# A state-space kernel on one core: GpSimd's product of C with an older state moves between the two halves of u times B

## The chip, the cores and the metric

The kernel runs on one core of one Trainium2 chip. The metric is device time in microseconds (us) of one execution. The engines are TensorE (PE; PEld is its weight load), VectorE (DVE), ScalarE (ACT), GpSimd (POOL) and SyncE (SP), whose queue issues the DMAs.

## The reference, cut to what matters

A layer norm of x (8 x 1024 tokens of 512) feeds a feed-forward part with fp4 rounding, which runs first and isn't touched, and a selective state-space (Mamba) part, which is the subject here. Its core is

```python
def step(h, inp):
    xt, dtt, Bt, Ct = inp
    dA = jnp.exp(dtt[:, :, None] * A[None])
    h = h * dA + (dtt * xt)[:, :, None] * Bt[:, None, :]
    y = jnp.einsum('bds,bs->bd', h, Ct)
    return (h, y)
```

with 1024 channels d, 16 states s and 1024 steps per sequence. Around it are an input projection, a convolution over 4 taps, a SiLU gate with z and an output projection; x and the feed-forward result are added.

## The kernel before

The state-space part is `phase_b`. Tokens are cut into 16 **chunks** of 512; two chunks make one sequence, so the first of a pair starts from state 0 (`hs<-decay,v` in the rows) and the second from a kept state (`hs<-decay,carry,v`). The two chunks of one pass of a hardware loop are called even and odd here. Chunks 0, 1, 14 and 15 are written out; 2 to 13 are six passes of the loop on every engine.

A chunk is 32 **slots** k = 0 to 31: 2 groups of 512 channels times 16 states. A slot is 4 **steps** n = 4k + j, one for each block of 128 channels. What each engine does, in an order fixed in the program:

- **GpSimd**, slot k (`drive`, L1184 to L1195): `v[k % 2]` = u times B, in two instructions of two blocks each (L1193), called the low half (j = 0, 1) and the high half (j = 2, 3) here. The low half waits for the row of B (`b_rep`, three buffers) and for scans 0 and 1 of slot k - 2, the high half for scans 2 and 3 of that slot. Then `weigh` (L1197 to L1205): `hw` = state of slot k - 2 times C for the last 128 tokens of the chunk (L1203), for 28 of the 32 slots (`WEIGHED`: not for 5, 9, 27 and 29). Last, in 10 of the slots, the steps of `POOL_AT`: in slots 3 and 4 `y2` (L1218, `sz<-acc,sz`) of the chunk before, in slots 7, 11, 29 and 31 `sp` (L1222) and `du` (L1228), in 22 and 23 `y2` of this chunk.
- **ScalarE**, step n: `decay` = exp(A dt) into one of three PSUM buffers (L1392), and between these the copies and functions of `ACT_AT`, among them the copy of `yt` (L1324) at step 13.
- **VectorE**, step n: the scan over 512 tokens (L1434), then for n - 5 the sum `acc` += turned state times C (L1448), where the state isn't weighed by GpSimd. The scan of step 4k waits until state buffer k % 3 is free: its old state must be turned by TensorE and multiplied by GpSimd (`weighed`). The old state is that of slot k - 3, but **at the head of a chunk that of slot 30 (for k = 0) and 31 (for k = 1)** of the chunk before, only two slots back. GpSimd multiplies these two in its slots 0 and 1.
- **TensorE**, step n: it turns state n - 4 (`ht`, L1579), then adds up a product of C (`yw`, L1589) of slot (n - 9)/4, then does its share of the projections by a list (`MM`). At step 10 comes `yt(1, 0)` (L1557), which needs `y2` of GpSimd's slot 3.
- **SyncE**: slot k issues the steps of `SP_AT`, then the row of C for slot k (L1089), then the row of B for slot k + 2 (L1083), which waits for both halves of v of the slot that used its buffer last. Slot 31 first issues `x_z` (L1118, 1 MB), which waits for TensorE, and then the B row of the next chunk's slot 1.

Of the kernel before, what the change touches and what calls it, by code (L numbers as in the profile page):

```python
# [821 lines left out]
def phase_b(nc, ctx, xn_d, xnt, res, ssm_d, tap_d, xc_d, halo_d, ident, out, W_in, conv_w, conv_b, W_x, A_log, D_param, dt_bias, W_out):  # L822
# [18 lines left out]
    NC, KH, CL = xnt.shape[0], xnt.shape[2], xnt.shape[3]  # L841
    DI, NS = A_log.shape
    D = W_out.shape[1]
    ND, GD, NT, KC = DI // P, 4, CL // P, conv_w.shape[2]
# [132 lines left out]
    def sums(c, k, t):  # L977

        return c.at(ADDS, max(i for (a, b), i in add_no.items() if b == t and a <= k) + 1)
# [18 lines left out]
    def whose(c, what, g=None):  # L998

        if what == "tr":  # L1000
            return c.plus(2)
        if what == "tr_late":
            return c.plus(1)
        if what in ("ip", "cv", "ssm", "ct", "silu_xc"):
            return c.plus(1)
        if what in ("abs", "exp", "ln", "relu", "sp", "du", "xd"):
            return c if g == 1 else c.plus(1)
        if what in ("wo", "yt", "y2", "silu_z", "add", "load", "store"):
            return c.plus(-1) if g == 1 else c
        return c  # L1010

    def is_first(o):

        return isinstance(o.q, int) and o.c == 0

    def wait(eng, sem_, value):

        if not isinstance(value, int) or value > 0:
            eng.wait_ge(sem_, value)  # L1019

    def over_chunks(eng, part, first=-1):

        for r in range(first, 2):
            part(Chunk(0, r))
        with eng.Fori(1, NC // 2 - 1) as q:
            part(Chunk(q, 0))
            part(Chunk(q, 1))
        for r in (0, 1, 2):
            part(Chunk(NC // 2 - 1, r))
# [151 lines left out]
    @block.gpsimd  # L1181
    def _(pool):

        def drive(c, k):  # L1184

            g = k // NS
            for j in range(0, GD, 2):
                if j == 0:
                    wait(pool, b_loaded[k % 3], c.at(16 * len(range(k % 3, SLOTS, 3)), 16 * (k // 3) + 16))
                if k % NS == 0:  # L1190
                    wait(pool, u_ready, c.at(8, 4 * g + j + 2))
                wait(pool, scanned, c.at(128, 4 * (k - 2) + j + 2))
                nc.gpsimd.tensor_tensor(v[k % 2][:, j:j + 2, :], u[g][:, j:j + 2, :],  # L1193
                                        b_rep[k % 3][:, :].unsqueeze(1).broadcast_to([P, 2, CL]),
                                        ALU.mult).then_inc(v_ready, 2)  # L1195

        def weigh(c, k):  # L1197

            w = weigh_no[k]
            wait(pool, c_loaded[w % 4], c.at(4 * NW, 16 * (w // 4) + 16))  # L1200
            wait(pool, w_turned, c.at(NW, w - 1))
            wait(pool, scanned, c.at(128, 4 * k + 4))
            nc.gpsimd.tensor_tensor(hw[w % 2][:, :, :], h[k % 3][:, :, LT * P:],  # L1203
                                    c_rep[w % 4][:, :].unsqueeze(1).broadcast_to([P, GD, P]),
                                    ALU.mult).then_inc(weighed, 1)  # L1205

        def extra(c, what, g, half):
            o = whose(c, what, g)
            if not o.exists(NC) or (what in ("sp", "du") and g == 0 and is_first(o)):
                return  # L1210
            j = 2 * half
            two = slice(j, j + 2)
            if what == "y2":
                wait(pool, z_ready, o.at(4, 2 * g + half + 1))
                wait(pool, summed, sums(o, NS * g + NS - 1, j + 1))
                if half == LT // 2:
                    wait(pool, yw_added, o.at(2, g + 1))
                nc.gpsimd.tensor_tensor(sz[:, two, :], acc[g][:, two, :], sz[:, two, :], ALU.mult).then_inc(y2_ready, 2)  # L1218
            elif what == "sp":
                wait(pool, sp_ops, o.at(16, 8 * g + 7 + half))  # L1220
                wait(pool, relu_set, o.at(8, 4 * g + j + 2))
                nc.gpsimd.tensor_tensor(dt[g][:, two, :], dt[g][:, two, :], u[g][:, two, :], ALU.add).then_inc(dt_ready, 2)  # L1222
            else:
                wait(pool, xc_ready, o.at(ND, GD * g + j + 2))
                if is_first(o):
                    pool.wait_ge(xc0_loaded[2], 16)
                wait(pool, dt_ready, o.at(8, 4 * g + j + 2))
                nc.gpsimd.tensor_tensor(u[g][:, two, :], dt[g][:, two, :], xc[:, GD * g + j:GD * g + j + 2, :],  # L1228
                                        ALU.mult).then_inc(u_ready, 2)

        def part(c):
            for k in range(SLOTS):
                if c.exists(NC):
                    drive(c, k)
                done, m = (c, k - 2) if k >= 2 else (c.plus(-1), k + SLOTS - 2)
                if done.exists(NC) and m in weigh_no:
                    weigh(done, m)
                for what in POOL_AT.get(k, ()):
                    extra(c, *what)

        over_chunks(pool, part)

    @block.scalar
# [410 lines left out]
```

## Time and profile before

| what | value |
|---|---|
| median of 3 runs | 5356.45 us (5354.84 to 5357.74) |
| the profiled execution | 5352.76 us, its span 5351.0 us |
| PE busy | 4918.7 us, 92% |
| DVE busy | 4686.7 us, 88% |
| POOL busy | 3950.9 us, 74% |
| ACT busy | 2777.2 us, 52% |

The feed-forward part takes the first 1750 us or so; there GpSimd is busy little. In the state-space part behind it, VectorE and GpSimd are each busy over 95% of the time. Rows of a timeline give the start in us from the span's start, the length in us, engine, line, operation, what it writes from what it reads, and in brackets the engine's idle time before it with what ended it. "x2" is two instructions in one row.

### The profile page before, as it was taken

The numbers are of one execution on the slowest core, as the hardware profiler recorded it, in microseconds if no ns is written. First come the engines' busy times: TensorE is split into PE (matmuls) and PEld (weight loads), VectorE is DVE, ScalarE is ACT, GpSimd is POOL, SyncE is SP. The second block draws the span as 40 slices with busy tenths as digits, with TensorE's granted clock in tenths as the row PEclk, the third lists the DMA queues.
The fourth block names the chain that finished last, engine by engine and source line by source line (L and its number), as shares of the span: only waits on it lengthen the run. The fifth ranks groups of instructions, "written<-read, shape, count | busy, mean of one in ns | idle before, by whom it ended". The sixth has DMA issues, their size and how long they took to land.

```text
span 5351.0 us, 80535 instructions
## 1 busy us (share of the span) xinstructions
PE 4918.7 (92%) x22532; PEld 3287.7 (61%) x22532; DVE 4686.7 (88%) x5835; ACT 2777.2 (52%) x4594; POOL 3950.9 (74%) x2047
## 2 busy tenths in 40 slices
PE   5899999999999799899999999989999999999967
PEld 2688888888888455555555555555555555555544
DVE  9676766767676699999999999999999999999997
ACT  3111111111111576777677677777667776767754
POOL 5233333333332599999999999999999999999996
PEclk9999999999999899999999999999999999999979
DMA  4111111111110423323233333333333333323222
GB/s 117 48 44 41 45 39 45 41 43 43 39 47 32 128 88 111 102 92 108 87 122 101 91 104 110 98 102 94 115 95 99 107 92 111 110 81 114 80 91 66
DMA packets 286369, 444.72 MB, mean 83 GB/s; under 512 B 39521, under 2 KB 100961, under 8 KB 281746
## 3 DMA queue, kind: packets, MB, share of 16 engines
q1 hardware_dynamic: 285970, 440.23, 26.2%
q8 instruction: 150, 2.46, 0.2%
q14 instruction: 249, 2.04, 0.1%
HBM read 350.94 MB, written 89.17 MB: 82 GB/s over the span
## 4 chain that ended last, share of the span: by engine, by line
DVE 18%; PE 17%; issue 14%; ACT 8%; POOL 7%; DVEq 1%; DMA 1%; SPq 0%; POOLq 0%; ACTq 0%
DVE hs L1434 11%; DVE acc L1448 6%; POOL v L1193 5%; PE mm L1567 4%; PE ht L1579 4%; ACT decay L1392 3%; PE mm L1508 3%; PE mm L1499 3%; PE mm L1516 2%; POOL hw L1203 1%; PE yw L1589 1%; PE mm L1551 1%; DVEq L1019 1%; DMA b_rep<-ssm_d 1%; ACT L1279 1%
## 5 line engine op out<-in xcount | busy, mean ns | idle before, releaser
L1193 POOL TENSOR_TENSOR v<-u,b_rep 128x1024 f32<-128x1024 f32 x1024 | 2401.2, 2365 | 150.2 <-DVE hs L1434 68.1
L1392 ACT ACTIVATE decay<-dt,a_neg 128x512 f32<-128x512 f32 x2048 | 1389.7, 688 | 657.0 <-DVE hs L1434 644.7
L1579 PEld LDWEIGHTS ht<-ident,hs 128*128 128x128 f32 x6400 | 784.8, 144 | 1013.9 <-issue 662.6
L1434 DVE TENSOR_TENSOR_SCAN hs<-decay,carry,v 128x512 f32<-128x512 f32 x1024 | 1285.2, 1273 | 34.9 <-POOL hw L1203 19.5
L1434 DVE TENSOR_TENSOR_SCAN hs<-decay,v 128x512 f32<-128x512 f32 x1024 | 1230.6, 1221 | 49.2 <-ACT decay L1392 38.3
L1448 DVE SCALAR_TENSOR_TENSOR acc<-ht,c_now,acc 128x512 f32<-128x512 f32 x1600 | 1173.3, 733 | 17.4 <-PE ht L1579 16.5
L1579 PE MATMUL ht<-ident,hs 128*128 128x128 f32 x6400 | 1005.0, 281 | 179.3 <-DVE hs L1434 83.6
L683 ACT ACTIVATE sg<-gate 128x512 f32<-128x512 f32 (+1 forms) x192 | 108.1, 563 | 1339.9 <-PE up L723 1339.9
L1203 POOL TENSOR_TENSOR hw<-hs,c_rep 128x512 f32<-128x512 f32 x448 | 572.1, 1277 | 10.4 <-DVE hs L1434 10.4
L1567 PE MATMUL mm<-w_out,yt 128*128 128x512 f32 x1024 | 513.0, 605 | 8.7 <-ACT xb L1264 5.2
L1516 PE MATMUL mm<-w_in,x_z 128*128 128x512 f32 x1024 | 508.6, 601 | 6.7 <-ACT acc L1318 6.7
L1499 PE MATMUL mm<-x_in,w_in 128*128 128x512 f32 x960 | 484.2, 613 | 3.1 <-ACT x_in L1286 2.7
L1508 PE MATMUL mm<-xb,tap_diag 128*128 128x512 f32 x960 | 467.0, 596 | 6.1 <-ACT rtb L1314 6.1
L106 POOL TENSOR_TENSOR h<-h,h_small 128x1408 f32<-128x1408 f32 x64 | 166.2, 2597 | 413.8 <-DVE h_small L100 413.8
L151 POOL TENSOR_TENSOR h<-h,h_small 128x1408 f32<-128x1408 f32 x64 | 166.4, 2600 | 335.3 <-DVE h L145 335.3
L1589 PE MATMUL yw<-ident,hw 128*128 128x128 f32 x1792 | 283.5, 283 | 57.6 <-DVE acc L1456 46.6
L721 PE MATMUL gate<-gu,xqt 128*128 128x512 f32 (+1 forms) x768 | 301.4, 392 | 5.8 <-DVE xqt L619 5.8
L628 DVE TENSOR_TENSOR rt<-down,rt 128x512 f32<-128x512 f32 x64 | 44.3, 692 | 297.8 <-PE down L723 297.8
L722 PE MATMUL gate<-gu,xqt 128*128 128x512 f32 (+1 forms) x768 | 289.9, 378 | 0.0
L723 PE MATMUL gate<-gu,xqt 128*128 128x512 f32 (+1 forms) x768 | 289.5, 377 | 0.0
L721 PE MATMUL up<-gu,xqt 128*128 128x512 f32 (+1 forms) x768 | 288.7, 376 | 0.0
L723 PE MATMUL up<-gu,xqt 128*128 128x512 f32 (+1 forms) x768 | 288.7, 376 | 0.0
(157 smaller groups left out, 7971.0 us busy)
## 6 DMA issues: line engine op xcount, KB each, us to landing
b_rep<-ssm_d SPq DMA_DIRECT2D x512, 256.0 KB, 3.5
w_out<-in_L_attn_W_out SPq DMA_DIRECT2D x32, 1024.0 KB, 7.8
rtb<-res_d SPq DMA_DIRECT2D x128, 256.0 KB, 4.1
tap_diag<-tap_d SPq DMA_DIRECT2D x120, 256.0 KB, 3.5
c_rep<-ssm_d SPq DMA_DIRECT2D x448, 64.0 KB, 3.4
xt<-in_L_attn_x SPq DMA_DIRECT2D x64, 256.0 KB, 2.7
xn_d<-xn SPq DMA_DIRECT2D x64, 256.0 KB, 2.0
rt<-in_L_attn_x SPq DMA_DIRECT2D x64, 256.0 KB, 2.6
```

The source lines that it names most:

```text
L721: nc.tensor.matmul(out, left_hi, right_hi, start=(k == 0), stop=False)
L723: last = nc.tensor.matmul(out, left_lo, right_hi, start=False, stop=(k == len(pairs) - 1))
L1193: nc.gpsimd.tensor_tensor(v[k % 2][:, j:j + 2, :], u[g][:, j:j + 2, :], b_rep[k % 3][:, :].unsqueeze(1).broadcast_to([P, 2, CL]), ALU.mult ...
L1203: nc.gpsimd.tensor_tensor(hw[w % 2][:, :, :], h[k % 3][:, :, LT * P:], c_rep[w % 4][:, :].unsqueeze(1).broadcast_to([P, GD, P]), ALU.mult) ...
L1392: nc.scalar.activation(decay[n % 3][:, :], dt[g][:, j, :], ACT.Exp, scale=a_neg[:, GD * g + j, s:s + 1]).then_inc(decay_ready, 1)
L1434: nc.vector.tensor_tensor_scan(h[k % 3][:, j, :], decay[n % 3][:, :], v[k % 2][:, j, :], carry[:, s, GD * g + j:GD * g + j + 1] if c.secon ...
L1448: nc.vector.scalar_tensor_tensor(out=acc[g][:, t, :], in0=ht[add_no[k, t] % 2][:, :, :].rearrange("p j d -> p (j d)"), scalar=c_now[c.r % ...
L1499: made, done = nc.tensor.matmul(bank[:, :], w_in[:, k, i * P:(i + 1) * P], x_in[:, k, :], start=first, stop=last), ip_done
L1508: made, done = nc.tensor.matmul(bank[:, skip:], tap_diag[i % 2][:, tap, :], xb[i % 2][:, tap + skip:tap + CL], start=first, stop=last), cv ...
L1516: made, done = nc.tensor.matmul(bank[:, :], x_z[:, k, t * P:(t + 1) * P], w_in[:, k, DI + g * GW:DI + (g + 1) * GW], start=first, stop=las ...
L1567: made, done = nc.tensor.matmul(bank[:, :], left, right, start=first, stop=last), wo_done
L1579: last = nc.tensor.transpose(ht[add_no[k, t] % 2][:, j, :], h[k % 3][:, j, t * P:(t + 1) * P], ident[:, :])
```

## The change

GpSimd's slot was low half, high half, product with C. It becomes low half, product with C, high half. Nothing is added or left out, and the waits of each instruction are the same as before.

```diff
-        def drive(c, k):
+        def drive(c, k, halves=(0, 1)):
             g = k // NS
-            for j in range(0, GD, 2):
+            for j in (2 * half for half in halves):
...
                 if c.exists(NC):
-                    drive(c, k)
+                    drive(c, k, (0,))
                 done, m = (c, k - 2) if k >= 2 else (c.plus(-1), k + SLOTS - 2)
                 if done.exists(NC) and m in weigh_no:
                     weigh(done, m)
+                if c.exists(NC):
+                    drive(c, k, (1,))
                 for what in POOL_AT.get(k, ()):
                     extra(c, *what)
```

## Rows read from the trace of the kernel before

**Rows 1.** Busy time in a stretch, with instruction counts, clock and DMA.

```profile
core 0: us, PE busy (x) PEld busy (x) DVE busy (x) ACT busy (x) POOL busy (x), PEclk, DMA share, GB/s
3100.00:3700.00 600.00, 553.80 (x2496) 324.77 (x2495) 584.20 (x631) 425.63 (x700) 578.72 (x286) 0.99 0.33 104
```

**Rows 2.** Waits, 1900 to 5100 us: total us, times, longest us.

```profile
DVE hs L1434 <- ACT decay L1392: 38.9, 35, 3.3
DVE hs L1434 <- POOL hw L1203: 22.7, 14, 2.7
DVE acc L1448 <- PE ht L1579: 8.9, 24, 1.2
DVE hs L1434 <- PE ht L1579: 8.9, 6, 2.0
SPq L1118 <- PE mm L1516: 152.2, 15, 11.3
```

**Rows 3.** GpSimd's instructions by line: busy us, mean ns, idle before.

```profile
L1193 POOL TENSOR_TENSOR v<-u,b_rep 128x1024 f32<-128x1024 f32 x1024 | 2401.2, 2365 | 150.2 <-DVE hs L1434 68.1 <-DVE u L1420 34.1 <-DMA b_rep<-ssm_d 29.1
L1203 POOL TENSOR_TENSOR hw<-hs,c_rep 128x512 f32<-128x512 f32 x448 | 572.1, 1277 | 10.4 <-DVE hs L1434 10.4
```

**Rows 4.** Timeline of GpSimd, slots 0, 1 and 3 of chunk 7.

```profile
3332.19 4.68 POOL L1193 TENSOR_TENSOR v<-u,b_rep 128x1024 f32<-128x1024 f32 x2
3336.82 1.27 POOL L1203 TENSOR_TENSOR hw<-hs,c_rep 128x512 f32<-128x512 f32 x1
3340.35 4.70 POOL L1193 TENSOR_TENSOR v<-u,b_rep 128x1024 f32<-128x1024 f32 x2 [2.26 <-DMA b_rep<-ssm_d]
3345.01 1.26 POOL L1203 TENSOR_TENSOR hw<-hs,c_rep 128x512 f32<-128x512 f32 x1
...
3357.95 2.37 POOL L1218 TENSOR_TENSOR sz<-acc,sz 128x1024 f32<-128x1024 f32 x1
```

**Rows 5.** Timeline of VectorE, same stretch: head of chunk 7, then step 13.

```profile
3335.57 0.74 DVE L1448 SCALAR_TENSOR_TENSOR acc<-ht,c_now,acc 128x512 f32<-128x512 f32 x1
3338.37 2.46 DVE L1434 TENSOR_TENSOR_SCAN hs<-decay,carry,v 128x512 f32<-128x512 f32 x2 [2.06 <-POOL hw L1203]
...
3346.55 2.46 DVE L1434 TENSOR_TENSOR_SCAN hs<-decay,carry,v 128x512 f32<-128x512 f32 x2 [1.41 <-POOL hw L1203]
...
3363.28 0.75 DVE L1448 SCALAR_TENSOR_TENSOR acc<-ht,c_now,acc 128x512 f32<-128x512 f32 x1 [0.32 <-PE ht L1579]
```

**Rows 6.** Timeline of TensorE, same stretch: steps 10 to 12.

```profile
3360.46 0.63 PE L1557 MATMUL mm<-ident,sz 128*128 128x128 f32 x4 [1.53 <-POOL sz L1218]
3360.92 1.88 PE L1499 MATMUL mm<-x_in,w_in 128*128 128x512 f32 x4
3362.64 0.60 PE L1579 MATMUL ht<-ident,hs 128*128 128x128 f32 x4
```

**Rows 7.** Timeline of SyncE's queue at the same chunk boundary.

```profile
3332.59 0.33 SPq L1118 DMA_DIRECT2D x_z<-xnt_d  x1
3333.10 0.33 SPq L1089 DMA_DIRECT2D c_rep<-ssm_d  x1
3333.75 0.33 SPq L1083 DMA_DIRECT2D b_rep<-ssm_d  x1
```

**Rows 8.** Timeline at chunk 15: VectorE at steps 0 and 14, ScalarE at step 13.

```profile
5099.75 2.46 DVE L1434 TENSOR_TENSOR_SCAN hs<-decay,carry,v 128x512 f32<-128x512 f32 x2 [2.05 <-PE ht L1579]
...
5121.79 0.60 ACT L1324 ACTIVATE yt<-mm 128x512 f32<-128x512 f32 x1 [2.32 <-PE mm L1557]
...
5124.63 1.28 DVE L1434 TENSOR_TENSOR_SCAN hs<-decay,carry,v 128x512 f32<-128x512 f32 x1 [0.40 <-ACT decay L1392]
```

**Rows 9.** Timeline of VectorE, head of chunk 8, where the loop jumps back.

```profile
3558.55 0.73 DVE L1448 SCALAR_TENSOR_TENSOR acc<-ht,c_now,acc 128x512 f32<-128x512 f32 x1
3562.34 2.34 DVE L1434 TENSOR_TENSOR_SCAN hs<-decay,v 128x512 f32<-128x512 f32 x2 [3.06 <-ACT decay L1392]
```

**Rows 10.** Timeline of GpSimd, TensorE and VectorE in slot 12 of chunk 8.

```profile
3643.77 1.27 POOL L1203 TENSOR_TENSOR hw<-hs,c_rep 128x512 f32<-128x512 f32 x1
3645.00 4.67 POOL L1193 TENSOR_TENSOR v<-u,b_rep 128x1024 f32<-128x1024 f32 x2
3645.10 0.66 PE L1589 MATMUL yw<-ident,hw 128*128 128x128 f32 x4 [0.28 <-POOL hw L1203]
...
3645.61 1.21 DVE L1434 TENSOR_TENSOR_SCAN hs<-decay,v 128x512 f32<-128x512 f32 x1
...
3651.74 0.75 DVE L1448 SCALAR_TENSOR_TENSOR acc<-ht,c_now,acc 128x512 f32<-128x512 f32 x1 [0.26 <-PE ht L1579]
...
3655.63 0.75 DVE L1448 SCALAR_TENSOR_TENSOR acc<-ht,c_now,acc 128x512 f32<-128x512 f32 x1 [0.24 <-PE ht L1579]
```

## The prediction

> **What bounds the kernel now.** I read the busy time by stretch first, to see which engines have no room in the state-space part; then the list of waits there, to see what the fullest engine waits for; then timelines around those waits, to see what comes next if one goes. In a stretch of 600 us VectorE is busy for 584.2 and GpSimd for 578.7 [rows 1]. VectorE sets the pace: whatever removes its 2.6% of idle time, and that alone, shortens the kernel. Of the idle time in 1900 to 5100 us, 22.7 us in 14 waits are put down to GpSimd's product `hw`, 38.9 to ScalarE's decay and 8.9 twice to TensorE's turned states [rows 2]. The scan waits put down to `ht`, 8.9 us, are the same thing under another name: in chunk 15 the scan of step 0 waits 2.05 us [rows 8], and it stands at the place where the wait for `hw` stands in chunk 7. So some 31.6 us lie behind the product of C. All of it is at the head of a chunk.
>
> **The waits at the head.** In chunk 7 VectorE's last sum begins at 3335.57 and takes 0.74, so it is free at 3336.31. GpSimd's slot 0 begins at 3332.19: two halves, then the product of slot 30, from 3336.82 to 3338.09. Scan 0 starts at 3338.37, after 2.06 us idle [rows 4, 5]. The semaphore takes 3338.37 - 3338.09 = 0.28. Scan 4 waits 1.41 us in the same way for the product of slot 31, which ends at 3346.27 [rows 4, 5].
>
> **What the change moves.** Two starts of GpSimd's instructions, 3332.19 and 3336.82, are 4.63 us apart, so a half costs 2.32; the product costs 1.23 by the starts 3643.77 and 3645.00 [rows 4, 10]. Its mean span is 1.28 [rows 3]. The slot's sum is the same, so GpSimd's slots begin when they began. Within a slot `hw` is ready 2.32 us earlier and the high half of v 1.23 us later.
>
> A sentence on the choice between 1.23 and 1.28: the Trainium skill, page "Perfetto Trace Analysis", section "GPSIMD Instruction", says that a GpSimd span isn't to be trusted and that starts should be compared. The trace agrees so far as the starts give the smaller number; with 1.28 in place of 1.23 the spare time below would be 0.05 us less, and the sum the same.
>
> **First part, the heads, and why I cost the gain at nothing.** New order in chunk 7: low half 3332.19 to 3334.5, product of slot 30 to 3335.8, plus 0.28 is 3336.0, before VectorE is free at 3336.31. So scan 0 gains 2.1 us. GpSimd's slot 1 can't start before 3340.35, since it waits 2.26 us for its row of B [rows 4]; its product now ends at 3340.35 + 2.32 + 1.27 = 3343.9. VectorE gets scan 4 at 3344.2, 2.3 us earlier than 3346.55, still after a wait of about 1.3. If nothing else held it, every such head would give 2.3 us.
>
> What is late next: `y2` in GpSimd's slot 3. It stands behind the whole of slots 1 to 3, so it runs from 3357.95 to 3360.32 as before. TensorE has been idle 1.53 us for it when it starts `yt(1, 0)` at 3360.46; then come four projection matmuls, and the turned state of slot 2 is finished at 3362.64 + 0.60 = 3363.24. VectorE's sum of step 13 starts at 3363.28, after an idle time of 0.32 us that ends with it [rows 4 to 6]. That chain is bound to the row of B in slot 1, and it holds VectorE already now. With VectorE 2.3 us ahead it waits 0.32 + 2.3 = 2.6 us there and goes on at 3363.28 as before. The gain of each head is handed back 13 steps later: 0. The same small wait stands at step 13 in chunks 1, 2, 3, 5, 7, 9, 13 and 14, from 0.26 to 1.2 us (they are most of the 8.9 us and hold the longest of the 24 waits of sums [rows 2]); in chunk 11 the turned state comes just in time.
>
> Chunk 15 has no such wait for the turned state, but a second tail of the same chain: ScalarE waits 2.32 us for `yt` of TensorE, then does its step 13, and scan 14 waits 0.40 us for its decay [rows 8]. So it is 0 there too.
>
> Where the loop jumps back (heads of chunks 4, 6, 8, 10 and 12), VectorE is idle for 3.06 us [rows 9] and the product isn't what ends it; moving the product brings 0.
>
> **Second part, slot 12 of the even chunks.** TensorE's `yw` waits 0.28 us for `hw` of slot 10 at 3645.10 (the product ended at 3645.04). VectorE's sums of steps 53 and 55 then wait 0.26 and 0.24 us for turned states [rows 10]. With `hw` 2.32 us earlier TensorE doesn't wait and is 0.3 to 0.45 us ahead, so the first of the two goes, and the second perhaps. The pair stands in chunks 2, 4, 8, 10 and 12, among the same 24 waits [rows 2]. Bounds: from 0 (another chain ends at the same time) to 0.50 a chunk. I take 0.3, nearer to the first wait's 0.26: 5 x 0.3 = 1.5 us gained.
>
> **Third part, the later high half.** It delays two users. The scans: the tightest place is slot 12 of an even chunk. Its high half ends with the pair, when `hw` starts: 3643.77 + 0.04 = 3643.81. Scan 50 starts at 3645.61 [rows 10]. 1.80 us are spare, of which 1.23 are used and 0.57 are left: cost 0. It can't bring a gain, since nothing here becomes ready sooner.
>
> The other user is SyncE, whose load of a row of B waits for the high half; behind it in the same queue are the row of C, the tap loads, residual rows, `x_z` and `w_out`. The row that GpSimd waits for at the head of each chunk is issued at 3333.75, right behind the 1 MB of `x_z` at 3332.59 [rows 7], and `x_z` has waited for TensorE for 152.2 us in 15 times, 10 us each [rows 2]. So 1.23 us later in the queue ahead of it is covered by those 10 us: cost 0. If that cover were gone it would cost 1.23 a chunk.
>
> **Sum.** 5352.76 (profiled execution, 1.8 over its span) - 0 - 1.5 + 0 = 5351.3. The median of the runs is 3.7 us above the profiled execution; I take the 1.5 off the median: 5356.45 - 1.5 = 5355.0.
>
> **The rivals.**
>
> *The heads' gain is kept (faster).* Ten heads (chunks 1, 2, 3, 5, 7, 9, 11, 13, 14 and 15) give up to 2.32 each, of the 31.6 us or so that are waited: 23 us, 5356.45 - 23 - 1.5 = 5332. For it: the waits for `hw` are the largest that the change touches, and they do go. Against it: `y2` and its 1.53 us of TensorE idle, and the 0.32 us at step 13, which show that the chain through GpSimd's slots 1 to 3 is late already. It would need that chain to begin earlier, that is, the row of B to land earlier. A part of it, if the row lands some 0.5 us earlier because `w_out` is issued later behind it: 10 x 0.5 = 5 us, 5350.
>
> *The rows of B come later (slower).* SyncE gets past its loads 1.23 us later in each slot. If this reaches the load for slot 1, GpSimd's slot 1, `y2`, the turned state and step 13 all shift by 1.23: 15 heads x 1.23 = 18.5 us, 5356.45 + 18.5 = 5375. It decides from the point where SyncE reaches `x_z` less than 1.23 us before TensorE is done; the row says 10 us.
>
> *The high half comes too late for scans 2 and 3 (slower).* It needs GpSimd's slots to be 0.57 us behind by slot 12. Slots 1 to 12 run back to back, so 0.05 us more in each slot would do it. At 0.1 a slot it would cost 0.6 us in each of 7 even chunks, 4 us: 5359. Against it: each slot has the same three kinds of hand-over between instructions as before (half to half, half to product, product to half), only in another order.
>
> **How the numbers follow.** Nothing much changes (5350 to 5360): 0.80. Heads' gain kept, wholly or by more than 11 us: 0.10; in a small part: 0.03. Rows of B late: 0.04. High half late: 0.03. A measurement of this kernel can tell about 0.2%, 10.7 us, from no change. Faster by more than that 0.10; slower by more 0.04, to which I add 0.02 for a high half later than worked out; within it 0.84. The range takes in the likeliest case with its bounds (0 to 2.5 us gained), 3 to 5 us of scatter, since the three runs lie 2.9 us apart, the small part of the first rival and the third: 5345 to 5362. The wholly kept gain and the late rows of B, 0.14 together, lie outside.
>
> **What would show it.** VectorE's waits put down to `hw` fall from 22.7 to below 10 us, and those of its sums for turned states grow from 8.9 to 25 or more, at step 13. In chunk 7, scan 0 follows the last sum without a gap, and scans from step 14 on stand as before relative to the end of `y2`. TensorE's wait for `y2` in that head grows from 1.53 to about 3.8 us. The two waits in slot 12 of chunk 8 shrink. GpSimd's wait for the row of B stays near 2.3. I am wrong if sums at step 13 don't wait longer (then the heads' gain is real), or if scans 2 of some slot wait for `v`.

## The result, and the profile after

The changed kernel is slower by a little. Its median is 5365.62 us (5361.79 to 5371.34, 22 runs) against 5356.29 us (5354.04 to 5357.80, 22 runs) for the kernel before: 9.3 us more, a ratio of 1.0018 with a 95% interval of 1.0011 to 1.0024. The slowdown is real, since the interval leaves out 1, and it lies just within the 0.2% that the prediction called no change. The predicted time of 5355.0 and its range of 5345 to 5362 miss it. The profiled execution took 5365.12 us, its span 5363.3 us, 12.3 us more than the span before.

Lines of the kernel after stand two further down, except GpSimd's: scans are L1436, sums L1450, turned states L1581, `yt` L1559.

First the busy time in the same stretch as [rows 1]. Both full engines lose about a microsecond in 600, and TensorE's granted clock falls from 0.99 to 0.98.

```profile
core 0: us, PE busy (x) PEld busy (x) DVE busy (x) ACT busy (x) POOL busy (x), PEclk, DMA share, GB/s
3100.00:3700.00 600.00, 553.19 (x2491) 325.18 (x2490) 583.03 (x629) 425.37 (x699) 577.88 (x285) 0.98 0.32 103
```

Then the waits of 1900 to 5100 us, as in [rows 2] (total us, times, longest us).

```profile
DVE acc L1450 <- PE ht L1581: 42.7, 11, 5.7
DVE hs L1436 <- ACT decay L1394: 39.6, 38, 3.2
PE mm L1559 <- POOL sz L1218: 38.9, 14, 4.1
DVE hs L1436 <- POOL hw L1203: 7.9, 9, 1.4
DVE hs L1436 <- PE ht L1581: 3.0, 2, 1.5
SPq L1118 <- PE mm L1518: 123.7, 14, 10.0
```

VectorE's scans waited 22.7 us for `hw` and 8.9 us for `ht` [rows 2]; now they wait 7.9 and 3.0. Of the 8.9, 5.9 us stood at heads and are the same event under another name; 3.0 us stand at step 88 of chunks 0 and 14, in both kernels. Its sums waited 8.9 us for turned states in 24 times; now they wait 42.7 us in only 11. The waits moved, as forecast, and grew on the way: 28.6 us for the product and 8.9 us for turned states became 7.9 us and 42.7 us. TensorE's wait for `y2` in the same stretch, 38.9 us, was this before:

```profile
PE mm L1557 <- POOL sz L1218: 18.7, 14, 2.0
```

Timeline of VectorE after, chunk 7, which answers to [rows 5]: the chunk's head and step 13. The head lies 5.1 us later in this execution than before, so only differences count.

```profile
3340.68 0.74 DVE L1450 SCALAR_TENSOR_TENSOR acc<-ht,c_now,acc 128x512 f32<-128x512 f32 x1
3341.32 2.46 DVE L1436 TENSOR_TENSOR_SCAN hs<-decay,carry,v 128x512 f32<-128x512 f32 x2
...
3349.34 2.46 DVE L1436 TENSOR_TENSOR_SCAN hs<-decay,carry,v 128x512 f32<-128x512 f32 x2 [1.25 <-POOL hw L1203]
...
3369.97 0.75 DVE L1450 SCALAR_TENSOR_TENSOR acc<-ht,c_now,acc 128x512 f32<-128x512 f32 x1 [4.22 <-PE ht L1581]
```

Timeline of GpSimd after, same head, which answers to [rows 4].

```profile
3345.47 2.37 POOL L1193 TENSOR_TENSOR v<-u,b_rep 128x1024 f32<-128x1024 f32 x1 [2.27 <-DMA b_rep<-ssm_d]
3347.80 1.26 POOL L1203 TENSOR_TENSOR hw<-hs,c_rep 128x512 f32<-128x512 f32 x1
...
3363.07 2.33 POOL L1218 TENSOR_TENSOR sz<-acc,sz 128x1024 f32<-128x1024 f32 x1
```

Timeline of TensorE after, same head, which answers to [rows 6].

```profile
3365.54 1.08 PE L1559 MATMUL mm<-ident,sz 128*128 128x128 f32 x4 [3.82 <-POOL sz L1218]
3366.42 3.08 PE L1501 MATMUL mm<-x_in,w_in 128*128 128x512 f32 x4
3369.33 0.60 PE L1581 MATMUL ht<-ident,hs 128*128 128x128 f32 x4
```

Read in this order they tell the whole case. Scan 0 follows the last sum with no gap (2.06 us before), scan 4 waits 1.25 us (1.41 before). GpSimd's slot 1 waits for its row of B as before, 2.27 us, and `y2` begins 3363.07 - 3345.47 = 17.60 us behind it, where [rows 4] give 3357.95 - 3340.35 = 17.60. So the chain that the prediction named begins no later and runs no slower up to `y2`. Behind `y2` it is slower. From the start of `yt(1, 0)` to the start of the turned state it is 3369.33 - 3365.54 = 3.79 us, where it was 3362.64 - 3360.46 = 2.18 [rows 6]. The same four instructions of `yt` take 1.08 us in place of 0.63 and the four of the projection 3.08 in place of 1.88.

The reason stands in the clock. First the kernel before, while TensorE waits for `y2` and right behind it:

```profile
3358.90:3360.40 1.50, 0.03 (x1) 0.00 (x0) 1.50 (x2) 1.50 (x3) 1.50 (x2) 1.00 0.76 210
3360.40:3362.60 2.20, 2.14 (x8) 1.21 (x9) 2.20 (x3) 1.42 (x3) 2.20 (x2) 1.00 0.05 18
```

and the kernel after, the same two stretches (the column behind POOL is the granted clock):

```profile
3361.50:3365.50 4.00, 0.22 (x3) 0.00 (x0) 4.00 (x5) 1.69 (x3) 4.00 (x3) 0.99 0.15 47
3365.50:3369.30 3.80, 3.76 (x8) 2.06 (x9) 0.25 (x1) 2.58 (x4) 3.80 (x3) 0.56 0.25 91
```

After an idle time of 1.5 us the matmuls ran at 1.00, which is 2.4 GHz; after 3.8 us they ran at 0.56, which is 1.2 GHz for nearly all of the stretch. VectorE was busy for 0.25 us of it: the slow matmuls lie on the path.

The ten heads where the product held VectorE, read from the two traces. "Waits" is the sum of VectorE's idle times ahead of scan 0, scan 4 and the sum of step 13 (in chunk 15 ahead of scan 14 too); "idle" is TensorE's idle time ahead of `yt(1, 0)`; "clock" is the granted clock in the 3.5 us behind it.

| chunk | waits before | after | idle before | after | clock before | after |
|---|---|---|---|---|---|---|
| 1 | 3.24 | 5.52 | 1.66 | 3.96 | 1.00 | 0.64 |
| 2 | 4.09 | 6.49 | 1.82 | 4.05 | 1.00 | 0.50 |
| 3 | 3.59 | 5.41 | 1.48 | 3.83 | 1.00 | 0.64 |
| 5 | 3.81 | 5.47 | 1.54 | 3.83 | 1.00 | 0.57 |
| 7 | 3.79 | 5.47 | 1.53 | 3.82 | 1.00 | 0.53 |
| 9 | 3.65 | 6.65 | 1.55 | 3.85 | 1.00 | 0.50 |
| 11 | 2.83 | 4.55 | 1.18 | 3.38 | 1.00 | 0.57 |
| 13 | 3.40 | 4.73 | 1.52 | 3.58 | 1.00 | 0.51 |
| 14 | 4.13 | 6.06 | 2.02 | 3.97 | 1.00 | 0.50 |
| 15 | 2.47 | 2.57 | 0.96 | 3.24 | 0.50 | 0.50 |
| sum | 35.0 | 52.9 | | | | |

The heads cost 17.9 us more in this execution and the span grew by 12.3. Two things went the other way. In slot 12 of the even chunks, of the two waits [rows 10] the first is gone and the second is 0.10 us, 5 x 0.40 = 2.0 us. And the first scan of the state-space part starts at 1790.8 us in place of 1792.1, 1.3 us earlier, ahead of all that the change touches. Some 2 us remain spread over the kernel, the size by which runs of one kernel differ. The heads of the even chunks 4 to 12, where the loop jumps back, didn't change: TensorE idles there 0.6 to 1.2 us ahead of `yt`, the clock behind it stays at 1.00, and VectorE still waits some 3 us for its first decay.

### The profile page after: what moved, and what is told of

The parts are those of the page before. It is cut to its first block, busy times and chain, and to the rows that moved or that the text cites. A ratio compares the mean times of both kernels' runs of the same rounds, so it can differ in the third digit from the quotient of the medians.

```text
span 5363.3 us, 80211 instructions
## 1 busy us (share of the span) xinstructions
PE 4922.6 (92%) x22532; PEld 3294.3 (61%) x22532; DVE 4683.5 (87%) x5835; ACT 2776.7 (52%) x4594; POOL 3952.4 (74%) x2047
## 4 chain that ended last, share of the span: by engine, by line
DVE 20%; PE 18%; issue 13%; ACT 8%; POOL 4%; DMA 1%; DVEq 1%; SPq 0%; ACTq 0%; POOLq 0%
DVE hs L1436 13%; DVE acc L1450 7%; PE ht L1581 4%; PE mm L1569 4%; PE mm L1501 3%; ACT decay L1394 3%; PE mm L1510 3%; POOL v L1193 2%; PE mm L1518 1%; DMA b_rep<-ssm_d 1%; PE yw L1591 1%; PE mm L1553 1%; DVEq L1019 1%; POOL hw L1203 1%; ACT L1281 1%
## 5 line engine op out<-in xcount | busy, mean ns | idle before, releaser
L1581 PEld LDWEIGHTS ht<-ident,hs 128*128 128x128 f32 x6400 | 787.7, 144 | 1012.4 <-issue 675.3
L1436 DVE TENSOR_TENSOR_SCAN hs<-decay,carry,v 128x512 f32<-128x512 f32 x1024 | 1285.1, 1273 | 19.1 <-ACT decay L1394 12.3
L1436 DVE TENSOR_TENSOR_SCAN hs<-decay,v 128x512 f32<-128x512 f32 x1024 | 1226.4, 1215 | 45.0 <-ACT decay L1394 38.8
L1450 DVE SCALAR_TENSOR_TENSOR acc<-ht,c_now,acc 128x512 f32<-128x512 f32 x1600 | 1168.2, 730 | 54.0 <-PE ht L1581 52.9
L1581 PE MATMUL ht<-ident,hs 128*128 128x128 f32 x6400 | 1004.6, 281 | 178.2 <-DVE hs L1436 82.6
```

The lines of the kernel that those rows point to most:

```text
L1436: nc.vector.tensor_tensor_scan(h[k % 3][:, j, :], decay[n % 3][:, :], v[k % 2][:, j, :], carry[:, s, GD * g + j:GD * g + j + 1] if c.secon ...
L1450: nc.vector.scalar_tensor_tensor(out=acc[g][:, t, :], in0=ht[add_no[k, t] % 2][:, :, :].rearrange("p j d -> p (j d)"), scalar=c_now[c.r % ...
L1581: last = nc.tensor.transpose(ht[add_no[k, t] % 2][:, j, :], h[k % 3][:, j, t * P:(t + 1) * P], ident[:, :])
```

## The experiments

**The theories.** *The clock theory*: the gain of the heads is handed back through `y2`, as predicted, and on top TensorE, which now idles 3.8 us for `y2`, does `yt` and the projection at half the clock, which costs 1.6 us and more in each of nine heads. *The first rival*: the chain of GpSimd itself is later, through rows of B or hand-overs. The trace speaks against it (17.60 in both). *The second rival*: the loss comes from the later high halves all over the chunk. In the expectations "theory" is the clock theory unless the words beside it name another. The kernel before ran beside each group of kernels with medians from 5355.74 to 5355.76 us; ratios are against it.

### Which slots carry the loss

**e2_heads_only**: the new order only in slots 0 and 1, which do the products of slots 30 and 31.

```diff
+                split = k < 2
                 if c.exists(NC):
-                    drive(c, k, (0,))
+                    drive(c, k, (0,) if split else (0, 1))
...
-                if c.exists(NC):
+                if split and c.exists(NC):
                     drive(c, k, (1,))
```

> The new order in slots 0 and 1 alone, the old order in all others. Nothing is left out. Theory (clock, at the heads): all of the loss is made there, and the gain of slot 12 is missing: 5365.6 + 2 = 5367 to 5369 us, sums at step 13 wait 4.2 us as in the changed kernel. Rival (the later high half or the later loads of rows cost in the other 30 slots): 5356 us or a little less.

Measured: 5368.37 us (5366.68 to 5372.62), ratio 1.0025 (1.0016 to 1.0035), as expected. The whole loss is there with two slots of 32 changed.

**e3_all_but_heads**: the same edit with `split = k >= 2`, the new order in the other 30 slots.

> The old order in slots 0 and 1, the new one in the other 30. Nothing is left out. Theory (clock, at the heads): no loss, and slot 12 of the even chunks gives 0.3 to 0.5 us in five chunks: 5354 us (5353 to 5355.5), TensorE waits for y2 as before (1.5 us in chunk 7). Rival (the other slots make the loss): 5362 us or more.

Measured: 5356.07 us (5353.05 to 5359.35), ratio 0.9999 (0.9990 to 1.0008). No loss is there; the small gain that was expected, 5353 to 5355.5, isn't seen either. The waits of the two kernels stand apart as they should. First e2_heads_only:

```profile
DVE acc L1451 <- PE ht L1582: 45.4, 18, 5.8
PE mm L1560 <- POOL sz L1218: 39.2, 14, 4.1
```

then e3_all_but_heads:

```profile
DVE hs L1437 <- POOL hw L1203: 23.7, 14, 3.4
PE mm L1560 <- POOL sz L1218: 19.5, 14, 2.0
DVE acc L1451 <- PE ht L1582: 8.7, 16, 1.2
```

The second is the kernel before in all three rows ([rows 2] have 22.7 and 8.9, and TensorE's wait was 18.7). So the later high halves of 30 slots cost nothing, and the second rival falls. VectorE has no wait left in slot 12 of chunk 8 in e3_all_but_heads, but the 1.5 us that this should bring can't be told from the scatter of runs.

### Is it the clock?

If the clock is the cause, TensorE at work while it waits should take the loss away, even if the work is useless. It costs nothing as long as it ends before `y2` does.

**e1_fill6**: six matmuls into the bank that `yt(1, 0)` is about to overwrite, in every head, ahead of the wait for `y2`.

```diff
             bank, first, last = mm[n % 2], unit == 0, unit == UNITS[what] - 1
+            if what == "yt" and args == (1, 0):
+                for i in range(6):
+                    nc.tensor.matmul(bank[:, :], ident[:, :], w_in[:, i % KH, 0:512], start=True, stop=True)
```

> The changed kernel, and TensorE does six extra matmuls (identity times a 128x512 piece of w_in, into the PSUM bank that yt(1, 0) writes right after) before it waits for y2 at step 10. Nothing is left out. Theory (clock): the changed kernel loses its time because TensorE's wait for y2 grows from 1.53 to 3.82 us and the granted clock behind it is 0.56 in place of 1.00, which makes the yt and projection matmuls of that head about 1.6 us longer. With six matmuls (2.6 us) in the wait the clock stays at 1.00 there, the sum of step 13 waits 2.6 us and not 4.2, and nine to ten heads give back 1.6 us each: 5365.6 - 15 = 5351 us. Rival (the chain through GpSimd is itself later, by its order or by the DMA of the row of B): the clock of TensorE doesn't matter, 5365 us.

Measured: 5386.69 us (5383.26 to 5387.78), ratio 1.0056 (1.0043 to 1.0070). A miss, and the timeline of TensorE in chunk 7 tells why:

```profile
3370.50 5.32 PE L1497 MATMUL mm<-w_in,ident 128*128 128x512 f32 x12
3375.65 0.60 PE L1562 MATMUL mm<-ident,sz 128*128 128x128 f32 x4
```

Each of these 32-bit matmuls stands as two instructions in the trace (x12 for six), so they take 5.32 us and not half of it. They fill the wait and run past it, in the heads of even chunks too, where only 0.6 to 1.2 us were free: at step 13 of chunks 4, 6, 8, 10 and 12 VectorE now waits 4.0 us each, 20 us, where it waited 0.3 at most. That is most of the 21 us by which this kernel is slower than the changed one. The clock behind the fill did stay at 1.00. The time says nothing on the theory, so the size was changed.

**e5_fill3_odd**: three matmuls, and only in odd chunks (`and c.second` added to the condition, `range(3)`).

> As e1, but three extra matmuls (e1's trace: twelve instructions in 5.32 us for six, so 2.7 us for three) and only at the heads of odd chunks, where the changed kernel's TensorE waits 3.2 to 3.9 us for y2. Nothing is left out. Theory (clock): TensorE is idle about 1.2 us in place of 3.8, its clock stays at 1.00, the sum of step 13 waits 2.6 us and not 4.2 or more; seven heads give back 1.6 us, chunks 2 and 14 are left as they are: 5365.6 - 11.5 = 5354 us (5352 to 5357). Rival (the chain itself is later in the changed kernel): 5365 us.

Measured: 5359.82 us (5357.03 to 5362.60), ratio 1.0008 (0.9999 to 1.0017). Windows of chunk 7, the wait with the fill and the stretch behind it:

```profile
3360.80:3364.60 3.80, 2.75 (x8) 0.97 (x6) 3.80 (x5) 1.65 (x3) 3.80 (x2) 1.00 0.13 41
3364.70:3367.20 2.50, 2.49 (x11) 1.48 (x12) 0.30 (x1) 1.73 (x3) 2.50 (x2) 1.00 0.41 147
```

and rows of TensorE and, last, VectorE at step 13:

```profile
3364.71 0.66 PE L1562 MATMUL mm<-ident,sz 128*128 128x128 f32 x4 [1.16 <-POOL sz L1218]
3365.21 1.88 PE L1504 MATMUL mm<-x_in,w_in 128*128 128x512 f32 x4
...
3367.56 0.75 DVE L1450 SCALAR_TENSOR_TENSOR acc<-ht,c_now,acc 128x512 f32<-128x512 f32 x1 [2.56 <-PE ht L1584]
```

The projection takes 1.88 us again. VectorE's wait at step 13 is 2.56 us, where the prediction had said 2.6 and the changed kernel has 4.22. It is 2.56 to 2.58 in all six odd chunks from 3 to 13. The heads of chunks 2 and 14, which were not, still wait 4.71 and 5.96 us at a clock of 0.55 and 0.50. In chunk 15 the fill changes little: its waits sum to 2.32 us in place of 2.57.

The time is a miss all the same: 5352 to 5357 was expected, and 5.8 us came back in place of 11.5. The heads aren't where it is missing. Their waits sum to 41.4 us by the trace, in place of 52.9, so they give back the 11.5. Two other places took some of it in this execution. Chunk 0, which has no fill, is 3.0 us longer than in the changed kernel's profile (e3_all_but_heads and e7_b_first show the same 3 us there, so it hangs on no fill; its cause is open). And in chunks 5, 7, 11 and 13 VectorE waits 0.4 to 0.7 us for a turned state at step 75; the kernel before has such waits in chunks 9, 11 and 13.

**e9_fill3_sel**: the three matmuls in the odd chunks up to 13 and in 14, and not in 15.

```diff
+            filled = (c.c in (1, 13, 14)) if isinstance(c.q, int) else c.second
+            if what == "yt" and args == (1, 0) and filled:
```

> As e5, but the three extra matmuls stand at the heads of the odd chunks 1 to 13 and of chunk 14, and not at the head of chunk 15. Nothing is left out. e5 came out at 5359.8, above what I expected; its trace puts the rest at the heads without cover (sum of step 13 waits 4.71 us in chunk 2 and 5.96 in chunk 14) and at chunk 15, where the matmuls came on top. Theory (the clock is all of the loss): chunk 14 gives back 1.7 to 2.6 us and chunk 15 about 2.5, chunk 2 stays: 5359.8 - 4.5 = 5355.3 us, no difference from the kernel before. Rival (a part of the loss has another cause, spread over the heads): 5359 us or more.

Measured: 5357.86 us (5351.70 to 5359.99), ratio 1.0002 (0.9993 to 1.0011). Its slowest run is below the fastest of the changed kernel, 5361.79. Twenty-four useless matmuls, three in each of eight heads, take the loss away as far as runs can tell. That is the direct evidence for the clock: nothing else was changed, the clock behind `yt` is 1.00 in all eight heads, and the wait at step 13 is 2.1 to 2.9 us in the seven odd ones, where 2.6 was forecast. It is also what the prediction's sum describes: all of the heads' gain handed back and nothing more. The time lies between the 5355.3 of the theory and the 5359 of its rival, so a part of up to 2 us with another cause isn't excluded. The head of chunk 2, which has no fill, accounts for 1.3 us of it: its waits sum to 5.3 us in place of 4.1 before. Between e5_fill3_odd and e9_fill3_sel the runs show no difference that can be told.

### Shortening TensorE's wait for y2

The theory says that the gain of the heads is real but is stopped at `y2`. Then `y2` earlier should set it free, and in the kernel before, where VectorE is held by the product first, it should bring little.

**e4_y2_slot2** moves the first `y2` from GpSimd's slot 3 to its slot 2 in the changed kernel, and **e6_y2_slot2_old** does so in the kernel before.

```diff
-    POOL_AT = {3: [("y2", 1, 0)], 4: [("y2", 1, 1)], 7: [("sp", 1, 0), ("du", 1, 0)],
+    POOL_AT = {2: [("y2", 1, 0)], 4: [("y2", 1, 1)], 7: [("sp", 1, 0), ("du", 1, 0)],
```

> The changed kernel, and the first y2 of the chunk before stands in GpSimd's slot 2 in place of 3, so 5.9 us earlier. Nothing is left out. Theory (the chain row of B, GpSimd's slots 1 to 3, y2, TensorE, step 13 hands the heads' gain back): TensorE doesn't wait for y2, its clock doesn't fall, the 2.3 us of ten heads are kept and the waits of 0.3 to 1.2 us at step 13 go too: 5356.3 - 23 - 3 - 1.5 = 5329 us (5325 to 5336). Rival (something else ends at the same time as y2, ScalarE's decay of step 14 or the scans' v, now 2.3 us later in slot 3): 5350 us or more.

> The kernel before, and the first y2 of the chunk before stands in slot 2 in place of 3, as in e4, without the changed order. Nothing is left out. Theory: the waits for the products of slots 30 and 31 (2.1 and 1.4 us in chunk 7) stay, since nothing there moves; only the waits at step 13 go, 0.26 to 1.2 us in eight heads, 3.9 us in all: 5355.8 - 4 = 5352 us. So e4's 26 us need both. Rival (e4's gain is that of y2 alone): 5330 us.

Measured: e4_y2_slot2 5329.65 us (5327.82 to 5331.43), ratio 0.9952 (0.9939 to 0.9966), and e6_y2_slot2_old 5351.56 us (5349.73 to 5355.70), ratio 0.9993 (0.9984 to 1.0002). Both times are as expected, though the 4 us of the second can't be told from no change. Waits of e4_y2_slot2, 1900 to 5100 us:

```profile
DVE hs L1436 <- POOL hw L1203: 9.2, 9, 1.3
DVE hs L1436 <- POOL v L1193: 7.3, 17, 0.7
DVE acc L1450 <- PE ht L1581: 0.7, 1, 0.7
```

and of e6_y2_slot2_old:

```profile
DVE hs L1434 <- POOL hw L1203: 23.8, 14, 3.2
DVE acc L1448 <- PE ht L1579: 8.4, 19, 1.2
```

In the new order the waits of VectorE's sums for turned states fall from 42.7 to 0.7 us. A new small one comes, 7.3 us for `v`. None of its 17 waits is near `y2`: they stand in slots 5, 8 and 12, and 13 of them are at a scan 2, which reads the high half. VectorE keeps its 2.3 us now, and it catches up with GpSimd. That fits the later high half beginning to count, whose cost was rightly put at 0 while the gain was handed back; no run here has the early `y2` without the later high halves and without the early row, so it isn't shown. In e8_y2_slot2_b_first below, where GpSimd is earlier too, no wait for `v` is left. In the old order the waits for `hw` stay at 23.8. There the waits at step 13 go wholly, as expected, but those of steps 53 to 55 and 75 to 77 grow, so that the sum is 8.4 us where it was 8.9.

### Taking away the wait for the row of B

**e7_b_first**: SyncE issues slot 31's row of C and the row of B for the next slot 1 ahead of `x_z`, which waits 10 us for TensorE, instead of behind it. So the chain itself begins earlier.

```diff
-             31: [("row", 3), ("x_z",)]}
+             31: [("row", 3)]}
...
                     load_b(c.plus(1), k + 2 - SLOTS)
+                if k == SLOTS - 1:
+                    move(c, "x_z")
```

> The changed kernel, and SyncE issues the rows of slot 31's C and of the next chunk's slot 1 of B before the 1 MB of x_z, not behind it. Nothing is left out. Theory (the chain begins with the landing of the row of B): GpSimd doesn't wait 2.3 us in slot 1, so slots 1 to 3 and y2 are 2.3 us earlier, TensorE waits 1.5 us for y2 and keeps its clock; the odd heads and those of 2 and 14 keep their gain: 5355.8 - 10 x 2.3 = 5333 us, and up to 1 us a head less for the wait for the product of slot 31: 5325 to 5335. Rival (the wait for the row of B isn't the start of the chain, another wait takes its place): 5350 us or more.

Measured: 5331.90 us (5326.50 to 5333.68), ratio 0.9952 (0.9938 to 0.9965), a time as expected. Its waits:

```profile
DVE acc L1452 <- PE ht L1583: 14.4, 16, 2.7
POOL v L1195 <- DMA b_rep<-ssm_d: 10.8, 14, 1.5
DVE hs L1438 <- POOL hw L1205: 0.4, 1, 0.4
```

GpSimd waits 10.8 us for rows of B where it waited 29.1 [rows 3]. With it goes scan 4's wait for `hw`, since that product stands in slot 1 behind the low half that the row had held up. The mechanism is only in part as expected. TensorE idles 2.3 us for `y2` in most odd chunks, where 1.5 were expected, and it doesn't keep its clock everywhere: VectorE waits 1.06 us at step 13 of chunks 3, 5 and 7, but 2.45 and 2.70 us in chunks 9 and 11. More on these two below.

**e10_b_first_old**: the same edit in the kernel before.

> The kernel before, and the rows of slot 31's C and of the next slot 1's B before x_z, as in e7, without the changed order. Nothing is left out. Theory: scan 0 still waits 2 to 2.7 us for the product of slot 30; the wait of scan 4, 0.3 to 1.4 us, falls to 0.5 or less; y2 is 2.3 us earlier, so step 13 doesn't hold VectorE: about 1 us for each of ten heads, 5355.7 - 10 = 5346 us (5342 to 5349), 14 us slower than e7. Rival (the row of B makes all of e7's gain, the order none): 5332 us.

Measured: 5338.37 us (5334.04 to 5340.97), ratio 0.9964 (0.9952 to 0.9976). A miss by 8 us: the earlier row is worth 17 us without the new order, not 10. By the trace two waits go, and they sum to 15 us, while scan 0's waits grow by 1 us in all. The rest of the 17 isn't accounted for. Scan 4's wait is gone in every head: 10.5 us in nine heads, of which chunks 2 and 14 alone had 2.73 and 1.74. And the row of B set the time of `y2` in this order as well, so the waits at step 13 went with it, 4.4 us; of the sums' waits of 8.9 us in all, 2.8 are left.

### Both, and the order's worth beside them

**e8_y2_slot2_b_first** has both edits on the changed kernel, **e11_y2_slot2_b_first_old** both on the kernel before, **e12_heads_y2_b** is the first with the new order only in slots 0 and 1.

> e4 and e7 together: the changed kernel, y2 in slot 2, the row of B before x_z. Nothing is left out. Theory: what e4 left at the odd heads is the wait of scan 4 for the product of slot 31, 0.8 to 1.6 us; with the row of B landed it falls to the 0.5 us of ScalarE's decay of step 5: 5329.7 - 8 x 0.7 = 5324 us. Rival (the row of B doesn't matter once y2 is early): 5330 us.

> e8 with the old order of GpSimd's slot: y2 in slot 2 and the row of B before x_z on the kernel before. Nothing is left out. Theory: the order alone makes the difference to e8, 2 to 2.3 us at each of ten heads: 5321.8 + 20 to 23 = 5343 us (5340 to 5346). Rival (the order is worth nothing once the chain is out of the way): 5322 to 5325 us.

> e8 with the new order in slots 0 and 1 alone, the old one in the other 30. Nothing is left out. It asks what the order is worth away from the heads. Theory (slot 12 of five even chunks gives 0.3 us each, the second part of the prediction): 5321.8 + 1.5 = 5323.3 us. Rival 1 (nothing): 5321.8. Rival 2 (the later high halves in e8 cost something by now): 5319 or less.

Measured: e8_y2_slot2_b_first 5321.83 us (5320.31 to 5322.88), ratio 0.9935 (0.9921 to 0.9948), 2 us better than expected. e11_y2_slot2_b_first_old 5338.97 us (5334.23 to 5340.48), ratio 0.9967 (0.9954 to 0.9979), a miss: 5340 to 5346 was expected. e12_heads_y2_b 5323.62 us (5321.88 to 5324.76), ratio 0.9939 (0.9926 to 0.9953), as expected. Waits of e8_y2_slot2_b_first, 1900 to 5090 us:

```profile
DVE acc L1452 <- PE ht L1583: 4.6, 10, 0.7
DVE hs L1438 <- POOL hw L1205: 1.0, 2, 0.5
```

and of e11_y2_slot2_b_first_old:

```profile
DVE hs L1436 <- POOL hw L1205: 14.2, 6, 2.7
DVE hs L1436 <- PE ht L1581: 7.5, 5, 2.0
DVE acc L1450 <- PE ht L1581: 3.1, 7, 0.7
```

With `y2` and the row out of the way the products still hold VectorE at the heads of the old order. Of the 7.5 us, 3.0 stand at step 88 of chunks 0 and 14 as in the kernel before; 4.5 and the 14.2 are at heads, 18.7 us. The new order leaves 1.0 us of them (its waits for `ht`, 4.2 us, are all at step 88). That is 17.7 us by the trace and 17.1 by the runs. The expectation had taken 20 to 23, 2 to 2.3 us a head; scan 0 waits that long in seven heads but only 0.8 to 1.7 us in chunks 1, 2 and 14. e8_y2_slot2_b_first is the best version, 34 us below the kernel before. The 1.8 us between it and e12_heads_y2_b fit the 1.5 us of slot 12, but they are no more than runs of one kernel differ by.

Medians in us, all eight together:

| | as it was | `y2` in slot 2 | row of B first | both |
|---|---|---|---|---|
| old order | 5356.29 | 5351.56 | 5338.37 | 5338.97 |
| new order | 5365.62 | 5329.65 | 5331.90 | 5321.83 |
| new minus old | +9.3 | -21.9 | -6.5 | -17.1 |

The same edit costs 9 us or brings 22, by what is late behind it. In the column where `y2` alone is earlier it brings 21.9 us, where the rival "the heads' gain is kept" has 23 and 1.5 for slot 12. That rival had priced the gain nearly rightly, and the waits for `v` may be what is missing. What it lacked was its condition, a `y2` that isn't late.

## Why the prediction was wrong, point by point

**What bounds the kernel, and the waits at the head: right.** VectorE's waits for the product are the ones that the change touches, and all are at heads. e2_heads_only and e3_all_but_heads show it from both sides. The working had two readings wrong, neither of which enters the sum: the waits for the product are 28.6 us and not 31.6, since 3.0 of the scans' waits for `ht` stand at step 88; and the waits at step 13 are 4.3 us of the 8.9, not most of them, the rest being 2.8 in slot 12, 1.7 at step 75 and 0.2 at step 13 of chunk 12.

**What the change moves: right.** `hw` is ready 2.3 us earlier in its slot: it starts 3347.80 - 3345.47 = 2.33 us behind the low half, where it was 4.66 [rows 4]. Scan 0's wait went wholly in chunk 7, and no head keeps more than 0.5 us of it. Scan 4 waits 1.25, where the working had 1.3.

**What is late next: right in place, wrong in size.** The chain over the row of B, slots 1 to 3, `y2`, `yt(1, 0)` and the turned state of step 13 takes the gain. TensorE's wait for `y2` grew from 1.53 to 3.82 us, where 3.8 was forecast. The step that failed is the sentence "With VectorE 2.3 us ahead it waits 0.32 + 2.3 = 2.6 us there and goes on at 3363.28 as before" and the 0 made of it. It took the time from `yt` to the turned state as a constant of 2.2 us, which it is only at the clock that TensorE had in [rows 6]. The idle time of 3.8 us was forecast, but not what TensorE does right behind it. It ran at half the clock, and the wait was 4.22 us: 0.32 + 2.3 + 1.6. In chunks 2, 9 and 14, where the low clock lasted over the next group of matmuls as well, the wait was 5.2 to 5.7 us. The term was 17.9 us over ten heads, and not 0. With three matmuls in the gap the wait measured 2.56 and the kernel 5357.86, so the rest of the step stands.

The trace of the kernel before held the warning, at the head of the same chunk 7. TensorE's first turned states there come behind an idle time of 2.32 us, and soon behind them four matmuls take 1.12 us that take 0.60 in [rows 6]:

```profile
3335.80 1.69 PE L1579 MATMUL ht<-ident,hs 128*128 128x128 f32 x8 [2.32 <-DVE hs L1434]
...
3341.53 1.12 PE L1579 MATMUL ht<-ident,hs 128*128 128x128 f32 x4 [0.56 <-DVE acc L1448]
```

```profile
3336.40:3343.10 6.70, 5.47 (x16) 3.18 (x16) 4.73 (x5) 3.63 (x6) 4.44 (x4) 0.50 0.84 316
```

The granted clock is 0.50 in the 6.7 us behind. So an idle time shorter than the forecast 3.8 us was already seen to be followed by the lower level.

**Chunk 15: nearly right.** The handing back by way of ScalarE's decay of step 14 was foreseen at 0. The waits there sum to 2.57 us against 2.47, but in another shape: 1.35 at step 13 and 1.22 ahead of scan 14. The clock was low there in both kernels, 0.50, so the change had nothing to lose in it.

**Slot 12 of even chunks: right.** In chunk 8 the first wait went, and the second fell from 0.24 to 0.10 us. By the trace it brings 2.0 us, forecast 1.5. No comparison of runs resolves it.

**The later high half: right.** Slot 12 of chunk 8 after, GpSimd's product with its next two halves, then VectorE's scan 50, as in [rows 10]:

```profile
3648.00 1.27 POOL L1203 TENSOR_TENSOR hw<-hs,c_rep 128x512 f32<-128x512 f32 x1
3649.23 4.68 POOL L1193 TENSOR_TENSOR v<-u,b_rep 128x1024 f32<-128x1024 f32 x2
...
3652.20 1.22 DVE L1436 TENSOR_TENSOR_SCAN hs<-decay,v 128x512 f32<-128x512 f32 x1
```

The high half begins at 3649.23 and takes 2.32, with the 0.04 of the prediction it is done at 3651.59, and scan 50 starts at 3652.20. So 0.61 us are left, where 0.57 were worked out. SyncE's cover held too: `x_z` waits up to 10.0 us for TensorE, and the row of B that GpSimd waits for is as late as before. e3_all_but_heads puts both at no cost in the time. This holds while VectorE hands the gain back; with the gain kept, in e4_y2_slot2, it waits 7.3 us for `v`.

**The rivals.** The two that ended slower, late rows of B and late high halves, didn't happen. The kernel was slower by a mechanism that stood in none of them. The prediction asked who waits for TensorE, and not in what state TensorE comes out of a longer wait. The bound for the heads' hand-back should have reached from 0 to what the matmuls behind `y2` take at the lower of the two levels, 2.2 us more a head, that is from 0 to 20 us over nine heads, and the range to 5375.

**The signs.** "Nothing much changes" was true to 0.2%. But it was believed for an exact cancelling of two sums of 23 us, and those are seldom exact.

## What to carry to other kernels

When an engine on the path waits for two things in turn, clearing the first moves its idle time to the second. On TensorE also ask how long that makes the idle time there, since the matmuls behind it may run at half the clock. If a gain is handed back further on, look for what can be moved out of that later chain, and value the edits together: here one cost 9 us by itself, was worth 17 to 22 with `y2` moved, and the pair that won was an edit of one number and an edit of one queue's order. A few useless matmuls in an idle gap, short enough to end within it, are a cheap way to see whether a loss is the clock's.

## What the runs showed of the hardware that was not expected

**A short idle time of TensorE can halve its clock right behind.** In the kernel before, idle times of 1.2 to 2.0 us ahead of `yt` left it at 1.00; in the changed kernel those of 3.4 to 4.1 us brought it to 0.50 to 0.64 in the 3.5 us behind, in all nine heads outside chunk 15. With the same wait filled by three matmuls (2.74 us busy, 1.16 us idle) it stayed at 1.00. The Trainium skill, page "TensorE: Matmul & The Clock Gate", section "Part 1: The HAM clock gate", tells of a gate that has just two states, 1.2 and 2.4 GHz, and that idle time throws it to the lower. The traces agree: the granted clock in these stretches is a mix of 0.50 and 1.00.

**In between, the same idle time does either.** In e7_b_first TensorE idles 2.27 us for `y2` in chunk 7 and 2.25 us in chunk 11. First chunk 7:

```profile
3351.95 0.63 PE L1561 MATMUL mm<-ident,sz 128*128 128x128 f32 x4 [2.27 <-POOL sz L1220]
3352.41 1.88 PE L1503 MATMUL mm<-x_in,w_in 128*128 128x512 f32 x4
```

then chunk 11, and the window that starts with its `yt`:

```profile
4227.28 1.09 PE L1561 MATMUL mm<-ident,sz 128*128 128x128 f32 x4 [2.25 <-POOL sz L1220]
4228.16 3.12 PE L1503 MATMUL mm<-x_in,w_in 128*128 128x512 f32 x4
```

```profile
4227.20:4231.20 4.00, 3.92 (x9) 2.15 (x10) 1.86 (x2) 2.73 (x5) 4.00 (x3) 0.57 0.28 97
```

The one runs at full clock and the other at half. Chunk 9 idles for the same 2.27 us as chunk 7 and has a granted clock of 0.68 in the 3.5 us behind, where chunk 7 has 1.00. What decides between them these runs don't show. For an estimate an idle time of that length is a chance of a loss and not a fixed price.

**Scan lengths.** The scans of slots 8 to 11 in the even chunks 2 to 12 take 1205 to 1207 ns in the mean in the profiles of e1 to e4 and e9 to e12, but 1239 to 1246 ns in those of e5 to e8, whichever the edit; the kernel before has 1238 and the changed one 1223. The pace of VectorE doesn't differ with it. Its busy time, in which overlaps count once, is 4683 to 4687 us in all these profiles, and the kernel before, run beside each group, kept its median within 0.02 us. So a difference of that size between the recorded lengths of single scans in two profiles is no effect of an edit; starts and gaps are what to compare. The cause is open.
